# The residual sum x1 is written to SBUF by DVE, and ACT's copy of it out of the PSUM bank is dropped

## What is computed

```python
# layer 0: linear attention over a raw and a 5x5-convolved branch, then a 1x1 projection
qkv = concat(h @ wq.T, h @ wk.T, h @ wv.T)
pw  = conv1x1_grouped(conv5x5_depthwise(qkv, dw_kernel), pw_kernel)
f   = concat(qkv, pw)                                  # query, key, value of 64 heads of 8
scores = einsum("bhdn,bhen->bhde", value_pad, relu(key))
out = einsum("bhde,bhen->bhdn", scores, relu(query));  out = out[:-1] / (out[-1:] + eps)
x1  = conv1x1(out, proj_kernel) * inv + (beta - mean * inv) + x       # residual sum

# layer 1: softmax attention over the 1024 pixels
norm = (x1 - mean(x1)) / sqrt(var(x1) + eps)
energy = (f_w @ norm + f_b).T @ (g_w @ norm + g_b)
out = (h_w @ x1 + h_b) @ softmax(energy).T
y   = o_w @ out + o_b + x1
```

## Time and profile before

| what | value |
|---|---|
| median of three runs | 700.99 us |
| lowest and highest run | 698.55 us, 703.51 us |
| span of the profiled execution, first to last instruction | 700.8 us |
| mean granted PE clock, share of full speed | 0.978 |
| busy: PE, DVE, ACT, POOL | 636.0, 563.5, 470.7, 541.0 us |

### The profile page before, as it was taken

One profiled execution on the slowest core, in us unless ns is written; L12 is line 12 of the kernel. 1 busy time (PEld: TensorE's weight loads), 2 busy tenths in 40 slices (PEclk: granted clock), 3 DMA queues, 4 the chain that ended last, 5 costly groups with the idle time before them and its releaser, 6 DMA issues.

```text
span 700.8 us, 8645 instructions
## 1 busy us (share of the span) xinstructions
PE 636.0 (91%) x3176; PEld 475.3 (68%) x3176; DVE 563.5 (80%) x661; ACT 470.7 (67%) x745; POOL 541.0 (77%) x253
## 2 busy tenths in 40 slices
PE   4979978999989999999989999999898977997998
PEld 3854537665868787656778877648677773485887
DVE  5899899788989999989999998989999993442321
ACT  4787608897777769888676977987886662232231
POOL 4899996999999899999999999999999891000000
PEclk9979999999999999999999999999999998899999
DMA  8000001001010000001100000000100000000000
GB/s 296 2 0 1 0 0 61 1 1 34 27 61 15 16 31 1 0 1 60 61 1 16 16 31 1 1 0 1 61 15 16 9 22 1 0 1 0 16 16 30
DMA packets 6537, 16.23 MB, mean 23 GB/s; under 512 B 864, under 2 KB 992, under 8 KB 5984
## 3 DMA queue, kind: packets, MB, share of 16 engines
q1 hardware_dynamic: 6496, 15.69, 6.3%
HBM read 11.50 MB, written 4.19 MB: 22 GB/s over the span
## 4 chain that ended last, share of the span: by engine, by line
PE 36%; issue 20%; DVE 16%; ACT 15%; POOL 12%; DMA 1%; POOLq 0%; SPq 0%; DVEq 0%; ACTq 0%
DVE ps L1143 9%; PE ps L629 7%; PE ps L605 7%; ACT prod L895 7%; POOL conv L1354 7%; POOL rows L1354 4%; PE ps L538 4%; PE ps L708 3%; DVE small L1280 2%; PE ps L471 2%; PE ps L620 2%; ACT raw L864 1%; PE ps L756 1%; PE ps L475 1%; PE ps L472 1%
## 5 line engine op out<-in xcount | busy, mean ns | idle before, releaser
L1354 POOL TENSOR_TENSOR conv<-conv,prod 128x930 f32<-128x930 f32 (+4 forms) x197 | 432.4, 2238 | 16.0 <-ACT prod L895 13.2
L1143 DVE SCALAR_TENSOR_TENSOR ps<-raw,dw_sb,ps 128x930 f32<-128x930 f32 (+4 forms) x295 | 354.1, 1201 | 7.6
L895 ACT ACTIVATE prod<-raw,dw_sb 128x930 f32<-128x930 f32 (+4 forms) x233 | 250.2, 1123 | 16.6 <-POOL conv L1354 16.6
L629 PE MATMUL ps<-ht,pt 128*128 128x256 f32 x512 | 115.4, 379 | 2.7 <-ACT pt L1050 2.7
L629 PEld LDWEIGHTS ps<-ht,pt 128*128 128x128 f32 x512 | 95.0, 190 | 14.8 <-ACT pt L1050 3.1
L1041 ACT ACTIVATE rows<-ps,small 128x1024 f32<-128x1024 f32 x32 | 35.6, 1113 | 82.2 <-DVE small L1284 82.2
L1354 POOL TENSOR_TENSOR rows<-rows,prod 128x930 f32<-128x930 f32 (+4 forms) x27 | 62.9, 2329 | 9.9 <-ACT prod L895 6.5
L1280 DVE TENSOR_REDUCE small<-ps 128x1 f32<-128x1024 f32 x32 | 39.1, 1220 | 27.9 <-PE ps L605 27.8
L605 PE MATMUL ps<-hi,t_hi 128*128 128x512 f32 x128 | 45.3, 436 | 14.4 <-ACT rows L1041 14.4
L471 PE MATMUL ps<-hi,wqkv_hi 128*128 128x512 f32 x92 | 38.9, 423 | 4.4 <-ACT vt L910 4.4
L605 PE MATMUL ps<-lo,t_hi 128*128 128x512 f32 x128 | 41.2, 404 | 0.0
(11 more groups left out here) (146 smaller groups left out, 1059.3 us busy)
## 6 DMA issues: line engine op xcount, KB each, us to landing
q_raw<-x_dram SPq DMA_DIRECT2D x8, 512.0 KB, 6.2
x<-x_dram SPq DMA_DIRECT2D x4, 1024.0 KB, 4.7
out_dram<-x_t SPq DMA_DIRECT2D x16, 256.0 KB, 2.3
conv<-wqkv_dram SPq DMA_DIRECT2D x1, 768.0 KB, 4.5
conv<-fg_dram SPq DMA_DIRECT2D x1, 512.0 KB, 5.1
proj_sb<-proj_dram SPq DMA_DIRECT2D x1, 512.0 KB, 7.6
pw_sb<-pw_dram SPq DMA_DIRECT2D x1, 384.0 KB, 6.1
mask_sb<-masks_dram SPq DMA_DIRECT2D x1, 264.0 KB, 6.2
```

What stands on the lines that cost most here:

```text
L629: mm = pe.matmul(dst[:, 0:C], pt[:, i % PT_BUFS, j, :], ht[:, j, :], start=(j == 0), stop=(j == NB - 1))
L895: act.activation(dst, view, ACT.Copy, scale=weight(t, i)).then_inc(prod_ready, 1)
L1143: return dve.scalar_tensor_tensor(dst, view, w, before, ALU.mult, ALU.add)
L1354: pool.tensor_tensor(total, total, product, ALU.add).then_inc(conv_pool, 1)
```

## The change

All four batches are changed alike. DVE writes the residual sum to x1 in SBUF at once. ACT's copy goes, and ACT rounds `hi` from x1 instead of from the bank. DVE forms `lo` from x1 instead of from the bank, so that both tensors that it reads now lie in SBUF. Waits and semaphores stay as they are, the bank still being given back behind `lo`. All other instructions keep their order on every engine; ACT's list is shorter by 16 copies, one for each of four units in four batches, and lines behind L992 move up by one.

```diff
                 for u, (c, h) in enumerate(UNITS):
                     cols = slice(h * HALF, (h + 1) * HALF)
                     act.wait_ge(x1_ready, D_PROJ * b + u + 1)
-                    act.copy(x1[:, c, cols], d_bank(D_AT["proj", b] + u))
-                    act.activation(hi[:, c, cols], d_bank(D_AT["proj", b] + u), ACT.Copy).then_inc(x1_hi, 1)
+                    act.activation(hi[:, c, cols], x1[:, c, cols], ACT.Copy).then_inc(x1_hi, 1)
                     products(PRODUCTS_X1[u])
...
                     dve.wait_ge(d_full, D_AT["proj", b] + u + 1)
-                    dve.scalar_tensor_tensor(bank, bank, bn_scale[:, c:c + 1], x1[:, c, cols],
+                    dve.scalar_tensor_tensor(x1[:, c, cols], bank, bn_scale[:, c:c + 1], x1[:, c, cols],
                                              ALU.mult, ALU.add).then_inc(x1_ready, 1)
...
-                    dve.tensor_tensor(lo[:, c, cols], bank, hi[:, c, cols].bitcast(F32),
+                    dve.tensor_tensor(lo[:, c, cols], x1[:, c, cols], hi[:, c, cols].bitcast(F32),
                                       ALU.subtract).then_inc(d_free, 1)
```

## The result

The changed kernel takes 707.37 us (median of 16 runs, 703.93 to 710.83) against 701.67 us (16 runs, 697.46 to 704.79). The ratio is 1.0087 with a 95% interval of 1.0063 to 1.0111: slower by 6.1 us (4.4 to 7.8; the two medians by themselves lie 5.7 us apart). The forecast, 705.3, was 4.3 us up; the measured time lies in its range.

The account below looks back on a forecast made before the run. In batches 0 to 2 the stage ends when DVE gets through the four units. Three stages 1.63 us late, less 0.59 gained in batch 3, make +4.3 us on 701.0: 705.3 us, range 698.5 to 711.

Parts of the forecast that it names:

- The contention: Batches 0 to 2: `lo` with two SBUF inputs waits for a running POOL add; 3.24 us instead of 1.29 in the trace.
- Unit 0: Batches 0 to 2: `lo` waits 1.09 us for a POOL add, less 0.48 gained by dropping the copy: +0.61 us.
- Unit 1: Batches 0 to 2: `lo`, asked for 0.61 us late, waits another 0.66 for an add; together +1.27 us.
- rstd: POOL, units 2 and 3: each `rstd` is kept out by `lo` for 0.36 us; the second is late by 1.63.
- The sum and the rounding: DVE's sum into SBUF and ACT's rounding from SBUF: small gains or losses either way, taken as nothing.
- Batch 3: No adds or taps: unit 3's sum moves up 0.11 us and its `hi` 0.48 more; gain 0.59 us.
- The sum: Whole kernel: 3 x 1.63 - 0.59 = +4.3 us on 701.0, giving 705.3 us; chance 0.65.
- No contention: Rival for `lo`: the subtraction does not contend with POOL's adds, only the copy counts; 699.0 us, chance 0.10.
- Starvation: Rival: overlapping adds leave `lo` of unit 0 no gap until POOL pauses by itself; +22.5 us, 723.5 us, chance 0.10.
- Part taken back: Rival: batch 0's late `rstd` need not make POOL late later, only two batches pay; +2.7 us, 703.7, chance 0.15.

Follow-up runs that it names:

- lo_psum: Changed kernel with `lo` reading the PSUM bank again (low part left wrong); ratio 0.997 against the kernel before, -2.1 us.
- lo_sbuf_alone: Kernel before with one input changed: `lo` reads ACT's copy in SBUF instead of the bank; ratio 1.0119 against the kernel before, +8.3 us.
- u01_sbuf: Changed kernel with `lo` of units 2 and 3 reading the bank; one run, changed stretch 38.64 us in batches 0 to 2, 37.21 in the kernel before.
- The two delay kernels: Kernel before with two or four spare statistics instructions ahead of `lo` of unit 0 in batches 0 to 2; ratios 1.0085 and 1.013.
- hi_psum: Changed kernel with ACT rounding `hi` twice, into the PSUM bank for `lo` and into SBUF for PE; ratio 0.9959 against the kernel before, 698.06 us.
- delay: Kernel before with two spare statistics instructions ahead of `lo` of unit 0 in batches 0 to 2; ratio 1.0085, +6.0 us.
- u23_sbuf: Changed kernel with `lo` of units 0 and 1 reading the bank; one run, changed stretch 36.82 us in batches 0 to 2, 37.21 in the kernel before.

## Why the prediction was right, step by step

- *The contention.* Right, and shown: lo_psum takes one input away and the whole loss goes; lo_sbuf_alone adds that input and nothing else and the loss is there. The Trainium skill's rule ("SBUF — State Buffer", section "Who interferes with whom") agrees with the trace at 1.81 and 1.61 us instead of 0.67. On the same page, section "SBUF: two separate sides", the Trainium skill says that the one that starts first holds what both need "for the whole instruction". That is a little long for the records here: `lo` began 0.12 us ahead of the add's recorded end.
- *Unit 0.* Forecast a `lo` of about 1.8 us, measured 1.81. *Unit 1.* Forecast 1.3, measured 1.61. This term was mis-sized, because the step before it was: the copy was priced at its own slot of 0.48 us, with units 1 to 3 covered by DVE's tap. lo_psum shows 0.65 per batch. In units 1 to 3 the tap did not quite cover ACT: before the change the statistics followed the start of their tap by 1.24, 1.24 and 1.25 us, in the changed kernel by 1.06, 1.09 and 1.12. For unit 1, before and after:

```profile
165.16 1.15 DVE L1143 SCALAR_TENSOR_TENSOR ps<-raw,dw_sb,ps 128x900 f32<-128x900 f32 x1
166.40 0.69 DVE L1232 BATCH_NORM_STATS2 stats<-x 128x6 f32<-128x512 f32 x1
```

```profile
162.39 1.15 DVE L1142 SCALAR_TENSOR_TENSOR ps<-raw,dw_sb,ps 128x900 f32<-128x900 f32 x1
163.45 0.68 DVE L1231 BATCH_NORM_STATS2 stats<-x 128x6 f32<-128x512 f32 x1
```

So `lo` of unit 1 came 0.50 us later than before instead of the forecast 0.61, further ahead of the end of its add, and waited 0.93 instead of 0.66. Earlier by a tenth, later by a quarter: that is the mark of a wait that ends at another engine's time. The adds behind the two were forecast at about 2.6 us and took 2.75 and 2.69.
- *rstd.* Forecast 0.36 us each, measured 0.38, and u01_sbuf shows that `lo` of units 2 and 3 does it. But the forecast put all of it on the way to the end, and only 0.23 of it got there (u01_sbuf). The forecast of 0.9 us idle ahead of the first `rstd` was 0.14 too high.
- *The sum and the rounding.* Taken as nothing; in the mean 0.746 against 0.755 us and 0.630 against 0.604. Right.
- *Batch 3.* Forecast 0.59 gained, measured 0.77. The forecast held that the sum of unit 2 stays where it is, since PE has just finished. But PE had itself been late with unit 2: the first weights of that unit waited for `lo` of unit 0 until 604.65. With that `lo` earlier, the sum of unit 2 moved up by 0.19 us (6.99 to 6.80), which is the missing part.
- *The sum.* Forecast 3 x 1.63 - 0.59 = +4.3; the stages of the profile give 3 x 1.66 - 0.77 = +4.2. That these agree to 0.1 us is in part luck. In a batch the copy gains 0.65 instead of 0.48, the two waits cost 2.08 (38.64 - 36.56) instead of 1.75, and `rstd` costs 0.23 instead of 0.36: three misses that nearly cancel. The runs give +6.1 with 4.4 as the lower end of their interval. What the sum lacked is some 2 us that don't stand in the changed stage and for which the prediction has no term. The two delay kernels have the same excess without any second SBUF input, so it does not belong to the contention. As far as these records show, it is time at the lower clock: the remainders of the profiles follow that time, and at equal clock the excess is within the noise. Why the later kernels were granted less was not shown, and single profiles of lo_psum and hi_psum, which end earlier, have more time at 1.2 GHz as well.
- *The rivals.* No contention: out. Starvation: out, since DVE gets in between two adds that overlap in the records. Part taken back: out. In the changed kernel POOL's later wait in batch 0 shrank from 2.29 us to 0.87, but from the last row maximum of batch 0 to the first sum of batch 1 it takes 63.65 us before and 63.68 after.

## What to carry to other kernels

Before moving a DVE operand from PSUM to SBUF, count the SBUF inputs of each instruction that reads it, and look at what POOL does at that time: one input in PSUM is a way past POOL, and it can be the other operand, as hi_psum shows. A wait of this kind is not in any list of waits. It is found by comparing the shortest and the longest duration of one form of instruction, as `lo` at 0.67 and 1.81 us, and by the neighbour on the other engine that grew. And time that is saved ahead of such a wait is mostly lost again: dropping the copy gains 0.65 us a batch where nothing waits (lo_psum against the kernel before) and 0.15 where `lo` waits (39.02 against 38.87), so its saving must not simply be added to the sum.

## What the runs showed of the hardware beyond that

- A step of one element per partition on POOL is kept out just like a large add: `rstd` 0.55 to 0.93 us, although it reads a single element of each partition. In u23_sbuf it takes 1.01 us behind a `lo` that is itself kept waiting (0.99 us).
- Start-up differed by up to 6 us between profiles: the first sum of batch 0 starts at 154.46 us in delay's profile and at 160.30 in that of the kernel before, while the changed stretch repeats to within 0.03 us. Stage lengths tell tenths of a microsecond apart where a single span can't tell 3 us.
